# Counting edges with a straight TensorE program: four region offsets in one load, constant waits, and source one-hots 632 wide

## The reference

```
e = einsum('ehd,ehd->eh', k[src], q[dst]) / sqrt(64)
m = segment_max(e, dst);  ex = exp(e - m[dst]);  z = segment_sum(ex, dst)
a = segment_sum((ex / z[dst])[:, :, None] * v[src], dst)
```

## Time and profile before

| | |
|---|---|
| median of 3 runs | 2011.01 us (2009.99 to 2012.26) |
| span of the profiled execution | 1920.3 us |
| median of the runs less the span | 90.7 us |
| busy in the span: PE, PEld, DVE, ACT, POOL | 1621.3, 1166.7, 976.6, 701.1, 557.3 us |
| mean granted TensorE clock | 0.914 of full speed |
| count_edges, first one-hot to last logarithms' start | 239.38 to 359.94 us |

### The profile page before, as it was taken

One profiled execution on the slowest core, in us unless ns is written; L12 is line 12 of the kernel. 1 busy time (PEld: TensorE's weight loads), 2 busy tenths in 40 slices (PEclk: granted clock), 3 DMA queues, 4 the chain that ended last, 5 costly groups with the idle time before them and its releaser, 6 DMA issues. The chain is left out here.

```text
span 1920.3 us, 32208 instructions
## 1 busy us (share of the span) xinstructions
PE 1621.3 (84%) x9860; PEld 1166.7 (61%) x9861; DVE 976.6 (51%) x1958; ACT 701.1 (37%) x1610; POOL 557.3 (29%) x637
## 2 busy tenths in 40 slices
PE   1992067799999889697999999947999999898994
PEld 0551023488888746453999999934555555655662
DVE  8320177676667557544000000067999999632233
ACT  0220034355555423343222221145555555441331
POOL 6777500110110022134000000044555555133133
PEclk6996567799999999798999999968999999998997
DMA  6200190110110050345666554065555555618985
GB/s 175 60 7 6 35 368 0 22 23 12 22 22 1 22 136 1 139 145 140 271 236 233 198 204 181 9 179 168 157 154 153 155 156 153 205 46 267 349 275 182
DMA packets 131139, 252.81 MB, mean 132 GB/s; under 512 B 35344, under 2 KB 52596, under 8 KB 126572
## 3 DMA queue, kind: packets, MB, share of 16 engines
q1 hardware_dynamic: 91692, 171.81, 26.8%
q0 software_dynamic: 39360, 79.86, 14.4%
HBM read 196.03 MB, written 55.52 MB: 131 GB/s over the span
## 5 line engine op out<-in xcount | busy, mean ns | idle before, releaser
L2018 PE MATMUL acc<-prod,ohy 128*64 128x256 f32 x1056 | 249.1, 386 | 6.9 <-DVE prod L2136 6.9
L2062 ACT ACTIVATE ohy<-oh,RECS 128x64 f32<-128x64 f32 x704 | 187.0, 336 | 151.4 <-PE acc L2018 151.4
L2018 PEld LDWEIGHTS acc<-prod,ohy 128*64 128x64 f32 x1056 | 138.3, 137 | 131.6 <-issue 70.0
L1995 POOL DMA_INDIRECT rows<-up_dram,idx x176 | 166.9, 948 | 144.0 <-DVE prod L2136 101.6
L689 PE MATMUL ps<-ohS,ohD 128*128 128x512 f16 x352 | 87.9, 400 | 114.5 <-DVE ohS L664 91.2
L269 POOL DMA_INDIRECT rec_dram<-recs,pos x157 | 160.2, 1021 | 60.1 <-issue 48.9
L2021 PE MATMUL acc<-prod,ohy 128*64 128x256 f32 x704 | 177.3, 395 | 0.0
L1772 DVE TENSOR_SCALAR FT<-y_ps,b2T 128x188 f32<-128x188 f32 x32 | 13.2, 413 | 319.1 <-PE y_ps L1721 319.1
L1709 PE MATMUL hid_ps<-FT,W 128*128 128x188 f32 x1024 | 168.3, 326 | 0.7 <-ACT FT L1746 0.7
L2136 DVE TENSOR_TENSOR prod<-w_ps,rows 128x768 f32<-128x768 f32 x176 | 166.4, 946 | 0.0
L1709 PEld LDWEIGHTS hid_ps<-FT,W 128*128 128x128 f32 x1024 | 165.8, 193 | 0.9 <-issue 0.9
(11 more groups left out here) (382 smaller groups left out, 2648.2 us busy)
## 6 DMA issues: line engine op xcount, KB each, us to landing
W<-in_L_ffn_w SPq DMA_DIRECT2D x16, 4096.0 KB, 15.7
bankW_sp<-in_L_ffn_W_sp SPq DMA_DIRECT2D x2, 4096.0 KB, 23.2
xin<-zeros SPq DMA_DIRECT2D x31, 256.0 KB
h_dram<-h3e SPq DMA_DIRECT2D x22, 256.0 KB, 4.5
h<-h_dram SPq DMA_DIRECT2D x22, 256.0 KB, 3.0
QF<-q_dram SPq DMA_DIRECT2D x20, 250.0 KB, 4.2
xin_sp<-zeros SPq DMA_DIRECT2D x17, 256.0 KB
xin_fq<-zeros SPq DMA_DIRECT2D x17, 256.0 KB
```

The costliest lines, as they stand in the source:

```text
L1995: pool.indirect_dma_start(out=rows[:, t, :], out_offset=None, in_=up_dram, in_offset=bass.IndirectOffsetOnAxis(ap=idx[:, par, t:t + 1], ax ...
L2018: upper = lambda m: nc.tensor.matmul(acc[0:HALFB, bank, :].rearrange("p (b c) -> p b c", c=MUL)[:, m:4:3 - m, :], ohs[:, 1 + m, :], pr[:, ...
L2062: last = nc.scalar.activation(ohy[:, t % OHY, i, :], oh[:, par, t, :], ACT.Copy, scale=RECS[:, bass.ds(BATCH * g + t, 1), 4 + i])
```

## The change

TensorE's loop over 22 turns becomes a straight program of 44 sets. Each set loads four ready offsets (region times 1,024) from a new table `spotI` of 176 integers with one load instruction and without a check of bounds, waits for `hot` against a constant, and issues the eight matmuls. The shifts, masks, the loop's counter and branch and TensorE's ticks are gone. The table takes two instructions on VectorE in front, a mask and a multiply, in place of a memset, the mask, a copy and seven multiply-adds. The source one-hots, and the row that they are compared with, are 632 columns wide in place of 625; the matmuls still read 625. Nothing changes in the loops of VectorE and GpSimd and in ScalarE's program.

```diff
-                        step(nc.vector.memset(region_of[:], 0))
-                        step(nc.vector.tensor_scalar(region_of[:, 0:GROUPS], blockI[:, 1:], REGIONS - 1, None, ALU.bitwise_and))
-                        in_word = region_of[:].rearrange("p (q k) -> p q k", k=WORD)
-                        step(nc.vector.tensor_copy(wordI[:], in_word[:, :, WORD - 1]))
-                        for k in reversed(range(WORD - 1)):
-                            step(nc.vector.scalar_tensor_tensor(out=wordI[:], in0=wordI[:], scalar=float(REGIONS), in1=in_word[:, :, k],
-                                                                op0=ALU.mult, op1=ALU.add))
+                        step(nc.vector.tensor_scalar(spotI[:], blockI[:, 1:], REGIONS - 1, None, ALU.bitwise_and))
+                        step(nc.vector.tensor_scalar(spotI[:], spotI[:], float(REGION), None, ALU.mult))
...
+            WIDEN = 632
...
-                nodes16 = sb("nodes16", [128, HALFN], F16)
+                nodes16 = sb("nodes16", [128, WIDEN], F16)
...
-                ohS, ohD = sb("ohS", [128, CRING, HALFN], F16), sb("ohD", [128, CRING, 2 * HALFB], F16)
+                ohS, ohD = sb("ohS", [128, CRING, WIDEN], F16), sb("ohD", [128, CRING, 2 * HALFB], F16)
...
-                        def region_in(regions, of):
-
-                            if of == 0:
-                                return regions & (REGIONS - 1)
-                            return (regions >> (2 * of)) & (REGIONS - 1)
-
-                        def sums(g, k, half, regions):
-
+                        for g in range(SETS):
+                            _, spots = nc.values_load_multi_w_load_instructions(
+                                spotI[0:1, SET * g:SET * (g + 1)], [mybir.EngineType.PE], min_val=0, max_val=(REGIONS - 1) * REGION,
+                                skip_runtime_bounds_check_because="the table holds a block number masked to the regions, times their size")
                             pe.wait_ge(hot, g + 1)
-                            pe.sem_inc(tick, 1)
                             for t in range(SET):
-                                slot = SET * k + t
-                                region = region_in(regions, SET * half + t) * REGION
+                                slot = (SET * g + t) % CRING
                                 for c0, cn in PARTS:
-                                    last = nc.tensor.matmul(ps[:, bass.ds(region + c0, cn)], ohD[:, slot, :],
+                                    last = nc.tensor.matmul(ps[:, bass.ds(spots[t] + c0, cn)], ohD[:, slot, :],
                                                             ohS[:, slot, c0:c0 + cn], start=False, stop=False, skip_group_check=True)
                             last.then_inc(counted, SET)
-
-                        def regions_of(word):
-                            return pe.value_load(wordI[0:1, bass.ds(word, 1)], min_val=0, max_val=REGIONS ** WORD - 1)
-
-                        with pe.Fori(0, WORDS) as r:
-                            regions = regions_of(r)
-                            for half in range(2):
-                                sums(2 * r + half, half, half, regions)
```

More of the change, by code:

```diff
@@ L35 @@
 SLOTS = ETILES * LANES
-WORD = 8
-WORDS = GROUPS // WORD
-assert WORDS * WORD == GROUPS and CRING == WORD
+assert GROUPS % 4 == 0 and CRING == 8
 EHID = 64
@@ L134, in gnn_moe_gnn_moe, with front @@
         low = sb("low", [128, GROUPS])
-        def front(KT, V, turnI, wordI, endI):
+        def front(KT, V, turnI, spotI, endI):
             with ExitStack() as st:
@@ L180, in front @@
                 odd, even = sb("odd", [LANES, GROUPS]), sb("even", [LANES, GROUPS])
-                region_of = sb("region_of", [LANES, GROUPS], I32)
                 fill = sb("fill", [LANES, ETILES // FILLS, REC])
@@ L567, in query_tiles, with count_edges @@
             return QS, tiles_scored, q_split, stage, split
-        def count_edges(LA, stage, split, turnI, wordI, endI):
+        def count_edges(LA, stage, split, turnI, spotI, endI):
             HALFN = NODES // 2
+            WIDEN = 632
             PARTS = [(0, 512), (512, HALFN - 512)]
-            SET = WORD // 2
+            SET = 4
             AHEAD, SETS = CRING // SET, GROUPS // SET
@@ L619, in _ @@
                         nc.gpsimd.memset(least[:], 2.0 ** -60)
-                        nc.gpsimd.iota(nodes16[:], pattern=[[1, HALFN]], base=0, channel_multiplier=0,
+                        nc.gpsimd.iota(nodes16[:], pattern=[[1, WIDEN]], base=0, channel_multiplier=0,
                                        allow_small_or_imprecise_dtypes=True).then_inc(numbered, 1)
@@ L2730, in gnn_moe_gnn_moe @@
             KT, V = sb1("KT", [128, HEADS, NODES], F32R), sb1("V", [P, TILES, DIM])
-            turnI, wordI = sb1("turnI", [128, GROUPS + 1], I32), sb1("wordI", [128, WORDS], I32)
+            turnI, spotI = sb1("turnI", [128, GROUPS + 1], I32), sb1("spotI", [128, GROUPS], I32)
             endI = sb1("endI", [128, BLOCKS], I32)
-            front(KT, V, turnI, wordI, endI)
+            front(KT, V, turnI, spotI, endI)
             LA = sb1("LA", [P, TILES, NODES])
             QS, tiles_scored, q_split, stage, split = query_tiles(attention)
-            count_edges(LA, stage, split, turnI, wordI, endI)
+            count_edges(LA, stage, split, turnI, spotI, endI)
             attend(KT, V, LA, FT, QS, tiles_scored, q_split, stage, split)
```

## The result

The changed kernel takes 1978.57 us (median of 4 runs, 1974.63 to 1983.88), beside 2011.28 us for the kernel before (4 runs, 2009.99 to 2012.26). The ratio is 0.9848, 95% interval 0.9827 to 0.987: 32.7 us less where 27 were forecast (1984.0 us).

What follows compares the result with a forecast made beforehand. TensorE's instruction issue in count_edges was taken as the bound; 43 intervals x 2.0 us plus 2.0, 1.9 and 3.7 gave 93.6 us against 120.6, so 2011.0 - 27.0 = 1984.0 us, range 1973 to 2008 (forecast's own 1975 to 1993).

Steps and rivals of the forecast that it cites:

- What bounds the kernel: In count_edges TensorE ends last at every step and lacks instructions, not data; 162.2 us of "issue" on its weight loads.
- Loop, waits, arithmetic: TensorE's sequencer in count_edges: removing these leaves eight matmuls at 1.04 us, a wait of 0.10 and the load per set.
- The load: TensorE's one load of four offsets per set in count_edges: 0.45 us quiet, 1.0 us under the zero fills.
- Rival A: Count_edges' load costs more per word, 0.9 us quiet and 2.2 under the fills: 2003 us; chance 0.13.
- rival B: Count_edges' load makes four separate trips, 1.21 us quiet and 2.92 under the fills: slower, 2016 us; chance 0.11.
- The array: TensorE's array in count_edges: 2.1 us a set at the lower clock, assumed for half the sets, 1.1 at the upper.
- VectorE the bound, 2.0 us a set: In count_edges VectorE becomes the bound at 1.85 to 1.9 us; sets average 2.0, about 2.05 under the fills, 1.95 after.
- Where the sequencer stands: Constant waits let TensorE's sequencer run some 3 us ahead, so a set costs the larger of sequencer, array and VectorE.
- rival E: Constant waits stop TensorE's sequencer in count_edges after all: 1.7 us a set, still under VectorE's; given no chance of its own.
- The sum: Count_edges: 86.0 + keys 2.0 + query split 1.9 + 3.7 is 93.6 us against 120.6; all 27 us reach the end.
- Rival C: No change within 4 us: load near 1.0 us quiet, or count_edges' about 1,150 instructions fetched during the fills; chance 0.09.
- Rival D: More gain in count_edges: array at the upper clock, VectorE at 1.75 or 1.6 us a set: 1973 or 1967 us; chance 0.05.

Runs made afterwards that it cites:

- four_loads: The changed kernel with four loads of one word a set in place of one load of four words; 2019.57 us, ratio 1.0056 to the kernel before.
- light_vector: The changed kernel with VectorE making only two of each set's four source one-hots, so counts are wrong; 1879.56 us in one run.
- loop_four: The changed kernel with TensorE's loop, register-valued waits and ticks put back, keeping the table and four-offset load; 1985.4 us, ratio 0.9878 to the kernel before.
- packed_straight: The kernel before with TensorE's program written out and constant waits, keeping packed words, shifts and the checked load; 1901.02 us, ratio 0.9902.
- narrow: The changed kernel with the source one-hots 625 columns wide again, nothing else; 1979.96 us, ratio 0.9857 to the kernel before.
- short_scatter: The changed kernel with front's GpSimd scatter covering 96 of 157 columns of records, so edges are missing; 1816.63 us in one run.
- before_again: The kernel before, unchanged, run for a second profile; 2008.13 us, ratio 1.0002.
- after_again: The changed kernel, unchanged, on another chip; 1891.69 us beside 1920.32 for the kernel before, ratio 0.985.

## Why the prediction was right, step by step

*What bounds the kernel.* Right, and shown from both sides: TensorE's instructions, not data. four_loads adds only sequencer time and loses all of the gain; light_vector takes away VectorE's work and finds that TensorE's side needs at most 1.40 us a set, below VectorE's 1.78. Of the rows given for it, the 31.1 us in which VectorE stood for TensorE bear it out; the 162.2 us of "issue" on the weight loads do not, as that row stays at 55.3 us after.

*Loop, waits, arithmetic.* Right. Forecast were 1.04 us for eight pairs, measured 0.95; the wait at 0.10 was near 0.12. The two halves, loop_four and packed_straight, gain 19.8 and 17.0 us of stage.

*The load.* The choice of a price near the one-word row was right, its size off: 0.332 us quiet where I took 0.45, a median of 0.822 and about 0.99 late under the fills where I took 1.0. The Trainium skill's figure of about 200 ns per register ("Runtime: NRT & Kernel Launch", section "Instruction fetch mechanics") does not hold here: 10 ns for each of words two to four, 0.26 us for the next four together. The page gives it for the registers of the runtime's own instructions; this table lies in SBUF. (Rival A's working with that figure gives about 1998 us, not 1999.) So rival A had no ground, and rival B's mechanism, four trips, was real but not in this form of the load: measured alone, it gives 2019.6 us, 3.6 from its forecast of 2016.

*The array.* Wrong in the level, by the row: half the sets were forecast at the lower clock. A set keeps the array for 1.23 us nearly throughout, the granted clock is 0.90 and 0.92, and in the stage the lower level shows only after TensorE had stood still: the first sets from 320.8 us, one behind the keys (16 matmuls in 3.67 us from 339.93), and three after the query split (24 matmuls in 6.04 us).

*VectorE the bound, 2.0 us a set.* The mean was 2.014 for the 43 intervals with keys and query split in it (86.6 us), where 86.0 + 2.0 + 1.9 = 89.9 had been forecast: 3.3 us of the 3.7 by which the stage was better. Most intervals are 1.78 us and not 1.85 to 2.1; eight late under the fills are 2.02 to 2.13, held by the load as forecast. The keys cost 2.0 us as said. The query split cost 2.7 and not 1.9: 391.06 to 395.53 on PE is 4.47 us. Five more intervals of 2.08 to 2.63 us stand at the start, behind the keys and behind the split, where the array ran at the lower clock. So 2.0 came near for a reason that was half wrong, and that is luck: it rested on a lower clock for half the sets. Without keys and split the mean is 1.90 us.

*Where the sequencer stands.* This reading of the earlier trace rows was wrong, without consequence. I took it that constant waits let the sequencer run ahead. In the changed kernel the load is read at 384.9 us, and the first register operations of the next set follow at 385.6, when its one-hots are done:

```profile
L668 PEldq TENSOR_LOAD <-spotI x1: 331/331/331, 384.9 to 384.9; - x1
L675 PEldq FUSED_REGOPS  x2: 42/44/46, 385.6 to 385.7; - x2
```

So the sequencer stands at the wait, as rival E had it. So the earlier trace rows did not show what I read from them. There the computations of line 2632 ran right behind the semaphore instruction of line 2630, which stands ahead of them:

```profile
L2630 PEldq EVENT_SEMAPHORE  x1: 51/51/51, 1843.1 to 1843.1; - x1
```

The sequencer had got through that wait, and was ahead of an array that was still busy with earlier matmuls; the rows don't show it passing a wait that was not yet met. E had priced this at nothing, and nothing it was: the matmuls start 0.14 us behind the last one-hot.

*Width and front.* Nothing, as said (narrow, short_scatter).

*The sum.* All of the stage's gain reaches the end: 29.5 us of stage, 27.1 of span, 29.6 of median between before_again and after, and 28.6 on the other chip. "90.7 us lie around the span" was wrong in its place: some 80 of them lie inside, in front, and on one kind of chip only. It was harmless since they stand in both kernels. "What ends the front is GpSimd's scatter" holds on the quick chips alone (short_scatter). *Rival C* (code fetched under the fills) did not come: the packets of the instruction queue q8 went from 51 to 55 and the matmuls' row has only 1.7 us of "issue" left in the whole stage. *Rival D*, VectorE's bare pace, holds for most sets: 43 x 1.78 + 2.0 + 2.7 and a tail of 3.3 are 84.5 us. The other 5.4 of the measured 89.9 are the eight sets under the late fills (2.2) and the five behind a pause of the array (3.15).

## What to carry to other kernels

When an engine waits for "issue", add up its sequencer's instructions one by one for a turn of the loop, and look again at each of them under the heaviest DMA traffic of the stage: the same load took 0.33 us quiet and 1.0 us late under the fills. Put ready values side by side in a table and take four of them with one load, not one each; eight with one load brought nothing more. Removing the sequencer's work pays only down to the next engine's pace: here either half of the change alone brought about six tenths of the whole (17.0 and 19.8 of 29.5 us), and what was left then was to move the fills away, not to shorten the program further.

## What the hardware showed beyond that

A profiled run takes its span plus 1.6 to 1.7 us (1976.11 and 1974.5, 2003.21 and 2001.6, 1891.69 and 1890.1), so I take a larger difference between a profile and the median of the runs as time inside another execution, not around it. On the chip of the longer runs TensorE gets one instruction per 1.4 us from about 88 to 242 us, with before's program and with the change alike (before_again, then after, then after_again on the other chip):

```profile
179.47 1.01 PE L418 MATMUL ps<-FT,Wqkv 128*128 128x512 f32 x1 [1.79 <-issue]
182.27 1.01 PE L418 MATMUL ps<-FT,Wqkv 128*128 128x512 f32 x1 [1.79 <-issue]
```

```profile
178.45 1.01 PE L410 MATMUL ps<-FT,Wqkv 128*128 128x512 f32 x1 [1.79 <-issue]
181.25 1.01 PE L410 MATMUL ps<-FT,Wqkv 128*128 128x512 f32 x1 [1.79 <-issue]
```

```profile
55.15 67.42 PE L410 MATMUL ps<-FT,Wqkv 128*128 128x512 f32 x192 [1.00 <-ACT FT L426]
```

A matmul every 2.80 us there, 192 in 67.42 us here, and front ends at 312.9 in place of 233.5 us. GpSimd's scatter runs during the stretch on both kinds of chip, so it alone is not the cause. The cause stays open: no run here tells it.
